# Two score banks instead of three in the full attention of a hybrid layer stack

## What is computed

```
q, k, v = projections of layernorm(x), 16 heads of 8 features, 2 sequences of 1024 tokens
s = q k^T * 8 ** -0.5
attn = exp(s - max(s)) / sum(exp(s - max(s)))
x = x + (attn v) Wo
```

## Time and profile before

| | us |
|---|---|
| median of 3 runs | 1204.31 |
| profiled execution, its own time | 1204.97 |
| its span in the profile | 1203.2 |
| first to last exponential, first full attention | 310.45 |
| first to last exponential, second full attention | 310.32 |
| TensorE matmuls busy over the span | 1051.9 (87%) |
| VectorE busy over the span | 864.4 (72%) |
| ScalarE busy over the span | 748.8 (62%) |

### The profile page before, as it was taken

One profiled execution on the slowest core, in us unless ns is written; L12 is line 12 of the kernel. 1 busy time (PEld: TensorE's weight loads), 2 busy tenths in 40 slices (PEclk: granted clock), 3 DMA queues, 4 the chain that ended last, 5 costly groups with the idle time before them and its releaser, 6 DMA issues.

```text
span 1203.2 us, 31909 instructions
## 1 busy us (share of the span) xinstructions
PE 1051.9 (87%) x13025; PEld 484.6 (40%) x13025; DVE 864.4 (72%) x1151; ACT 748.8 (62%) x1510; POOL 90.4 (8%) x370
## 2 busy tenths in 40 slices
PE   7598999794587999899999998779898899999986
PEld 3344545442253333334444344442333334344443
DVE  3553654345554799899999944555999999999635
ACT  2422545237213389889999982231888899999921
POOL 8000100000000000000000000000000000000000
PEclk9897999888778999999999997789999999999978
DMA  3473432100006322220101000044313201001000
GB/s 96 138 211 72 98 92 74 39 1 1 0 0 189 86 64 63 55 51 18 29 19 24 24 20 10 1 124 140 71 44 72 53 18 25 22 18 30 18 15 35
DMA packets 73825, 64.97 MB, mean 54 GB/s; under 512 B 27792, under 2 KB 53648, under 8 KB 73552
## 3 DMA queue, kind: packets, MB, share of 16 engines
q1 hardware_dynamic: 73680, 62.94, 20.0%
HBM read 27.06 MB, written 35.85 MB: 52 GB/s over the span
## 4 chain that ended last, share of the span: by engine, by line
DVE 43%; PE 38%; DMA 7%; issue 4%; ACT 4%; SPq 3%; DVEq 0%; ACTq 0%
DVE nmf L1331 35%; PE wide L556 24%; PE bank L556 14%; DMA KQs<-m_dram 4%; ACT xcsq L949 2%; DVE xcsq L1148 1%; DVE res L1148 1%; SPq L378 1%; DVE nmt L1290 1%; ACT big L949 1%; SPq L309 1%; DVE big L1410 1%; SPq L299 1%; DVE x L1148 1%; DMA qf_dram<-big 1%
## 5 line engine op out<-in xcount | busy, mean ns | idle before, releaser
L1331 DVE TENSOR_REDUCE nmf<-wide 128x1 f32<-128x1024 f32 x512 | 587.3, 1204 | 40.4 <-PE wide L556 40.3
L949 ACT ACTIVATE big<-wide 128x512 f32<-128x512 f32 (+1 forms) x703 | 403.4, 601 | 81.1 <-PE wide L556 54.7
L556 PE MATMUL wide<-big,KQs 48*128 48x512 bf16 (+1 forms) x1376 | 349.4, 344 | 4.3 <-DVE nmf L1331 3.3
L556 PE MATMUL bank<-big,V 128*9 128x128 f32 x8192 | 319.9, 274 | 12.5
L556 PE MATMUL wide<-KQs,big 50*128 50x512 bf16 (+1 forms) x1035 | 266.9, 324 | 11.9 <-DMA KQs<-m_dram 10.8
L556 PEld LDWEIGHTS bank<-big,V 128*9 128x9 f32 x8192 | 176.8, 90 | 233.7 <-ACT big L949 221.7
L949 ACT ACTIVATE big<-bank 128x512 f32<-128x512 f32 (+2 forms) x473 | 233.8, 516 | 23.2 <-PE bank L556 10.6
L556 PE MATMUL bank<-KQs,big 50*128 50x512 bf16 x341 | 130.3, 382 | 6.8 <-DMA KQs<-m_dram 6.8
L556 PEld LDWEIGHTS wide<-KQs,big 50*128 50x128 bf16 x1035 | 70.6, 95 | 117.9 <-ACT big L949 56.5
L1296 DVE TENSOR_REDUCE nmw<-wide 95x4 f32<-95x512 f32 (+1 forms) x96 | 61.2, 640 | 58.9 <-PE wide L556 57.9
L949 ACT ACTIVATE xcsq<-xcsq 128x512 f32<-128x512 f32 x32 | 20.1, 630 | 124.2 <-DVE xcsq L1148 124.2
(11 more groups left out here) (175 smaller groups left out, 833.3 us busy)
## 6 DMA issues: line engine op xcount, KB each, us to landing
o_dram<-big SPq DMA_DIRECT2D x128, 64.0 KB
big<-kf_dram SPq DMA_DIRECT2D x32, 200.0 KB
kf_dram<-big SPq DMA_DIRECT2D x24, 256.0 KB, 4.2
qf_dram<-big SPq DMA_DIRECT2D x24, 256.0 KB, 4.0
KQs<-qf_dram SPq DMA_DIRECT2D x32, 192.0 KB
ow_dram<-scr SPq DMA_DIRECT2D x32, 142.5 KB
big<-kw_dram SPq DMA_DIRECT2D x16, 275.0 KB
kw_dram<-scr SPq DMA_DIRECT2D x12, 352.0 KB, 5.7
```

Of the source, the lines that this page charges most:

```text
L556: return nc.tensor.matmul(o, l, r, start=start, stop=stop, **kw)
L949: return nc.scalar.activation(o, i, f, **kw)
L1331: nc.vector.tensor_reduce(nmf[:, (s0 + i) % 4, c:c + 1], wide[:, k:k + 2, :].rearrange("p g c -> p (g c)"), AX.X, ALU.max, negate=True).th ...
```

## The change

Score tiles of the pass for the weights go through banks 4 and 5 in turn (SBUF = 2) and no longer through 4, 5 and 6. TensorE's wait before tile n is now for exponential n-2. No instruction is added, removed or moved on any engine: each engine's program has the same instructions in the same order, with other bank addresses, and one more wait, before tile 2 of the first unit. Bank 6 is not used in this part of a full attention; the projections before it still use banks 4 to 6.

```diff
@@ -40,6 +40,7 @@
 AHEAD = 3
 PTS = 8
 LAG = 4
+SBUF = 2
 AHEAD_W = 5
@@ -798,10 +799,10 @@
                     if t == 0:
                         pe.wait_ge(nm_in[(s0 + i) % 8], 16 * ((s0 + i) // 8 + 1))
-                    if n >= 3:
-                        pe.wait_ge(sc_exp, n - 2)
+                    if n >= SBUF:
+                        pe.wait_ge(sc_exp, n - SBUF + 1)
                     q0, k0 = S * b + 512 * y, S * b + P * t
-                    mm(bk(4 + n % 3), kop[r:r + KR + 2, p, k0:k0 + P],
+                    mm(bk(4 + n % SBUF), kop[r:r + KR + 2, p, k0:k0 + P],
                        qop[r:r + KR + 2, p, q0:q0 + 512]).then_inc(sc_ready, 1)
@@ -1069,7 +1070,7 @@
-                    fn(ptf[:, n % PTS, :], bk(4 + n % 3), ACT.Exp, scale=SCALE).then_inc(sc_exp, 1)
+                    fn(ptf[:, n % PTS, :], bk(4 + n % SBUF), ACT.Exp, scale=SCALE).then_inc(sc_exp, 1)
```

## The result

The changed kernel took 1225.45 us (median of 4 runs, from 1221.29 to 1232.18), the kernel before 1204.38 in the same comparison: ratio 1.0196, 95% interval 1.0134 to 1.0258, that is 1.3 to 2.6% slower. The forecast was 1234, with 1219 to 1255 as the range. The profiled execution took 1226.88 us, 21.9 more than that of before.

The account below looks back on a forecast made before the run. VectorE was taken as the bound at 4.62 us a unit, TensorE close behind; the longer loop makes it 4.86. 113 units at 0.24 us (27) plus 2 gave 1204.97 + 29 = 1234 us, range 1219 to 1255.

Parts of the forecast that it names:

- The bound: In the full attentions, VectorE sets the pace at 4.62 us a unit; TensorE alone needs 4.56, 0.06 less.
- the sum: Over both attentions: 113 units at 0.24 us are 27, plus 2 for some thirty units at TensorE's pace: 29 us.
- The longer loop: Even tile, its exponential, the odd exponential, next step's odd tile, value products, next even tile: 2.43 us for two steps.
- The alternation of 0.22 and 0.44 us: On TensorE, odd tiles of steady units stand alternately 0.22 and 0.44 us behind their even tiles.
- VectorE's loop: Maxima group half, reduction, half reusing its banks two steps later: some 1.7 us, 1.99 available, so it does not bind.
- The copy of bank 7: ScalarE's copy, awaited by value products, made one step in four 0.20 us longer; costed at nothing, uncovered 23 us.
- The slow release: Rival: every bank hand-over from exponential to waiting tile costs 0.14 us, not 0.05; 1254 us, chance 0.14.
- VectorE still covers it: Rival: the loop is really under 2.31 us for two steps, so not slower; 1205 us, chance 0.07.
- The clock: Rival: more gaps on TensorE bring more stretches at granted clock 0.51 in the attentions; 1256 us or more, chance 0.04.
- the units set by the DMA: 15 of 128 units whose next maxima are late from DRAM; they hide the loss, put at 0 us.
- The sign that I named for VectorE: In the profile after, VectorE idles before its reductions, some 0.24 us a unit; busy 40 of 40 us would refute.

## Why the prediction was right, and where its size was off

**The bound** was read rightly in its two numbers, VectorE at 4.62 us a unit with TensorE 0.06 us behind, but not in which of them ruled. Of the 102 ordinary units 69 were under 4.60 us before, most of them 4.57, TensorE's pace, and the sum had some thirty. VectorE fell behind by 0.05 us in each of them until the next long unit. It was the closeness of the two, and not any engine's share of the span, that made a small new wait count.

**The mechanism** is shown. The longer loop was put at 2.43 us for two steps and measured 2.44; a unit at 4.86 and measured 4.88. Runs changed its parts: the odd tile's wait alone brings all of the loss, the even tile's a quarter of it in ordinary units, and ScalarE's spacing and length come in once each (the shorter exponentials). The alternation of 0.22 and 0.44 us between even and odd tiles was seen as 0.24 and 0.45, though not everywhere (0.34 twice at the end of an attention). That VectorE's loop does not bind is shown by the units without maxima. The copy of bank 7, put at nothing, did cost nothing: the 4.88 us hold one.

**The slow release** (1254 us) fell: the odd tile's release took 0.05 us. The 0.14 us of its row exists, but at tiles that wait for two semaphores. **VectorE still covers it** (1205 us) fell with the 2.44. **The clock** stayed at 1.00 with two banks; that it could fall was no idle fear, as one bank shows.

**The term that was mis-sized** is that of the units set by the DMA. I put them at 15 and at 0 us, "a unit set by the DMA hides the loss". There were 24 long ones, and they shrank by 7.3 us. Of these, 1.0 us is the unit with the fall of the clock, which did not come back in the changed kernel, and 1.0 is of the six units with VectorE's reciprocal; the other 17 gave 5.3. The ordinary units gave 29.6 us, against the 29 of the sum. That this is so close is partly luck: there were 102 of them and not 113, but they started from 4.59 us on the mean and went to 4.88, 0.29 each and not 0.24. Had I set the term of the long units to -7, the forecast would have been 1227. These rows of SyncE show one of them, the seventh unit of the first attention, before (its first exponential starts at 439.80, the next unit's at 445.47):

```profile
441.57 0.51 SPq L299 DMA_DIRECT2D m_dram<-nmt  x1
442.13 0.46 SPq L411 DMA_DIRECT2D KQs<-m_dram  x1
```

and after (437.12 and 442.37):

```profile
438.78 0.51 SPq L300 DMA_DIRECT2D m_dram<-nmt  x1
439.33 0.46 SPq L412 DMA_DIRECT2D KQs<-m_dram  x1
```

The fetch was issued 442.13 - 439.80 = 2.33 us into this unit in the kernel before and 2.21 in the changed one. Over the four units up to it the issue came at 2.17, 2.23, 2.28 and 2.33 us before, and at 2.17, 2.21, 2.21 and 2.21 after: VectorE no longer falls 0.05 us further behind TensorE with every unit (the second attention has the same 2.33 and 2.22). That is 0.12 us of the 0.42 by which this unit shrank. The other 0.30 is the fetch itself, 2.87 us before and 2.57 after in the chain of waits:

```profile
439.33 2.57 DMA KQs<-m_dram
```

I put this down to the transfers of the next heads' operands, which go ahead of the fetch in the same queue and had 0.31 us more since the unit before; that part is argued and not tested. The run with the fetch ahead shows only that the issue behind the transposition is a large part of why these units are long: with three banks it takes 11.6 of the 20.0 us by which those 17 exceed 4.57.

**The sign that I named for VectorE** was half wrong. It should have idled 0.24 us a unit and did not by its busy time; "still busy 40 of 40" stood in my list of what would refute the forecast, and 39.66 came with the forecast right. A count of instructions would have been the right sign.

## What to carry to other kernels

- With fewer buffers between two engines, write down for each item which finished item it now waits for, and follow the loops over both engines back to the start, over two rounds as well. By the terms each loop over one buffer was hidden here (1.08 against 1.09 us, a margin too small to build on); the one that binds goes through both buffers and the work queued behind the second wait.
- It was not the number of banks that counted here but whose turn waits for whom. The odd tile, with the value products right behind it in the queue, needed the slack; for the even tile giving it up cost a quarter as much.
- A stage that already waits for something else gives part of a slowdown back. Count such units apart, and ask what their wait is anchored to.

## What was not expected of the hardware

- A score tile that waits for one semaphore started 0.05 us after the exponential's end, one that waits for two 0.14 us after, of which 0.05 is a semaphore instruction of its own on TensorE's queue.
- With one score bank the granted clock was 0.51 through both attentions (719 us each), though TensorE's matmuls covered 543.83 us of the first: its share of busy time, 76%, does not look idle, and is so high only because each matmul lasts longer at 1.2 GHz.
